# One signal of TensorE for each expert step, and expert outputs in two PSUM banks

## The reference

```python
g = t @ gate_w.T + gate_b                      # t: 2816 x 192 normed tokens, 16 experts
vals, idx = jax.lax.top_k(g, 4)
w = jax.nn.softmax(vals, axis=-1) / K
full_w = zeros((T, E)).at[arange(T)[:, None], idx].set(w)
h = jnp.einsum('th,ehf->tef', t, w1) + b1      # 192 -> 384 (gate and linear half)
h = _swiglu(h)                                 # min(g,7) * sigmoid(1.702 g) * (clip(l)+1)
y = jnp.einsum('tei,eih->teh', h, w2) + b2     # 192 -> 192
out = jnp.einsum('teh,te->th', y, full_w) * K
```

## Time and profile before

| what | us |
|---|---|
| median of 3 plain runs | 689.53 (689.51 to 690.78) |
| profiled execution, span from first to last instruction | 774.6 |
| busy in it: PE, DVE, ACT, POOL | 435.0, 574.6, 541.6, 456.0 |
| start of the first and of the last hidden product | 467.8, 721.3 |
| last copy of `y_ps` begins | 735.1 |

### The profile page before, as it was taken

The page is one execution under the profiler, slowest core; times in us unless marked ns, Lnnn a source line. Parts: engine busy times, 40 slices in busy tenths (PEclk is TensorE's granted clock), DMA queues, the critical chain, the costliest instruction groups (busy, mean ns, idle before and its releaser), DMA issues.

```text
span 774.6 us, 14447 instructions
## 1 busy us (share of the span) xinstructions
PE 435.0 (56%) x3943; PEld 289.1 (37%) x3943; DVE 574.6 (74%) x1466; ACT 541.6 (70%) x905; POOL 456.0 (59%) x554
## 2 busy tenths in 40 slices
PE   0794343645546364464642223775787787868544
PEld 0242132333324233242331222554565555546333
DVE  3787897799998999989888853565576665656746
ACT  0065898999998989999897622454666666667564
POOL 9781726237488888978878546455455454545510
PEclk9998555555555555555555556777999899999769
DMA  9469999998002021210010115532544443441078
GB/s 185 52 145 307 318 318 294 317 298 243 6 28 77 29 77 45 67 36 20 26 35 25 35 54 114 109 82 78 116 105 90 88 90 86 106 88 45 2 273 327
DMA packets 149613, 93.65 MB, mean 121 GB/s; under 512 B 77122, under 2 KB 143643, under 8 KB 149538
## 3 DMA queue, kind: packets, MB, share of 16 engines
q1 hardware_dynamic: 139266, 75.04, 38.1%
q0 software_dynamic: 10272, 17.70, 7.1%
HBM read 23.61 MB, written 61.24 MB: 110 GB/s over the span
## 4 chain that ended last, share of the span: by engine, by line
ACT 32%; SPq 17%; PE 16%; issue 12%; another core or an unknown queue 9%; DVE 8%; POOL 2%; DMA 2%; DVEq 0%; ACTq 0%; POOLq 0%
SPq L483 7%; PE pX L1927 4%; PE pS L1911 3%; PE pP L1911 3%; SPq L475 3%; ACT S_sq L1015 2%; ACT L1015 2%; PE pX L1681 2%; ACT S_sq L1010 2%; ACT stage L1060 2%; ACT S_u L886 2%; ACT S_sq L987 2%; ACT pTs L992 2%; SPq L432 2%
## 5 line engine op out<-in xcount | busy, mean ns | idle before, releaser
L782 POOL DMA_INDIRECT expert_rows<-stage,dest x118 | 118.7, 1006 | 124.2 <-ACT stage L1045 48.7
L1600 DVE TENSOR_SCALAR arena<-pS 128x512 f32<-128x512 f32 x59 | 40.7, 689 | 74.8 <-remote 49.9
L1927 PE MATMUL pX<-w2s,stage 128*128 x472 | 64.4, 269 | 44.1 <-ACT stage L1045 39.9
L706 POOL DMA_INDIRECT region<-rows,slots x60 | 68.1, 1135 | 16.3 <-issue 15.7
L597 POOL TENSOR_TENSOR w1s<-stage,w1s 128x384 f16<-128x384 f32 (+8 forms) x72 | 59.5, 826 | 11.0 <-ACT w1s L866 5.8
L1927 PEld LDWEIGHTS pX<-w2s,stage 128*128 128x128 f16 x472 | 43.1, 105 | 60.5 <-issue 57.3
L1681 PE MATMUL pX<-arena,WA 128*128 128x384 f16 x86 | 34.4, 502 | 42.5 <-ACT arena L878 29.5
L1803 PE MATMUL pP<-idb,S_p 128*88 128x128 bf16 x192 | 25.8, 316 | 54.3 <-DVE S_p L1418 54.3
L1053 ACT ACTIVATE arena<-pS 64x256 f32<-64x256 f32 x59 | 22.1, 375 | 48.7 <-remote 16.5
L706 POOL DMA_INDIRECT region<-arena,slots x36 | 42.9, 1191 | 16.1 <-issue 8.4
L752 POOL CAST oq<-o 128x384 bf16<-128x384 int8 x24 | 25.3, 1056 | 45.5 <-ACT o L970 45.5
(11 more groups left out here) (445 smaller groups left out, 1688.5 us busy)
## 6 DMA issues: line engine op xcount, KB each, us to landing
region<-zrow SPq DMA_DIRECT2D x45, 800.0 KB
w1s<-expert_rows SPq DMA_DIRECT2D x16, 384.0 KB, 7.4
stage<-in_L_ffn_w_dram SPq DMA_DIRECT2D x24, 192.0 KB
stage<-in_L_ffn_w_dram SPq DMA_DIRECT2D x8, 384.0 KB
w2s<-expert_rows SPq DMA_DIRECT2D x8, 384.0 KB, 11.8
arena<-in_x_dram SPq DMA_DIRECT2D x4, 672.0 KB
expert_rows<-stage,dest POOLq DMA_INDIRECT x118
out_dram<-xsel SPq DMA_DIRECT2D x8, 198.0 KB
```

The lines of the kernel that those rows point to most:

```text
L706: pool.indirect_dma_start(region_rows, bass.IndirectOffsetOnAxis(ap=slots[q % 3][:, i, m:m + 1], axis=0), rows[q % 3][:, i, :].bitcast(I16 ...
L782: pool.indirect_dma_start(y_dram, bass.IndirectOffsetOnAxis(ap=dest[(st - 7) % 8][:, j:j + 1], axis=0), ysb[b][:, j, :], None, bounds_chec ...
L1600: dve.tensor_scalar(lin[r], hidLC[r], -6.0 * XS * WS, 8.0 * XS * WS, ALU.max, ALU.min).then_inc(s["l_done"], 1)
L1927: ins = pe.matmul(y_ps[:, j, :], lhs, w2s[:, kind, bass.ds(k_, 1), :].rearrange("p o f -> p (o f)"), start=n == 0, stop=n == 4)
```

## The change

PE's three signals on the windows go. One signal, `products_done`, stands behind everything that a slot does, on the last output product (or on the last hidden one, where the slot has no output products). Every reader of `h_ready`, `hl_ready` and `mm2_done` now waits for `products_done` with the slot's number. The two gelus then wait for the same count, so the second wait goes. From block `Y_APART` = 7 on, outputs of odd blocks go to `pO` and those of even blocks to `pX` (`y_ps(n)`); before that all go to `pX`. From block 8 on, PE waits for the copy of two blocks before. At block 7, the first in `pO`, PE waits for `own_ready` 2, since `pO` holds the last group's table till then. The number and order of matmuls, copies and DMAs is the same.

```diff
-        y_ps = pX[:, 0:2 * C].rearrange("p (j c) -> p j c", j=2)
+        y_banks = [bank[:, 0:2 * C].rearrange("p (j c) -> p j c", j=2) for bank in (pX, pO)]
+        def y_ps(n):
+            return y_banks[n % 2 if n >= Y_APART else 0]
...
+        Y_APART = SPREAD_AT
...
 # SP, load_step
-                    sp.wait_ge(s["hl_ready"], p - (UNROLL - 1))
+                    sp.wait_ge(s["products_done"], p - (UNROLL - 1))
...
 # ACT, gate_values
-                    act.wait_ge(s["mm2_done"], p - 5)
+                    act.wait_ge(s["products_done"], p - 2)
...
-                    act.activation(ysb[b], y_ps, ACT.Copy, scale=1.0 / (XS * WS * WS)).then_inc(s["y_out"], 1)
+                    act.activation(ysb[b], y_ps(st - 6), ACT.Copy, scale=1.0 / (XS * WS * WS)).then_inc(s["y_out"], 1)
                 if active(st, 2):
-                    act.wait_ge(s["h_ready"], p * 2 - 3)
+                    act.wait_ge(s["products_done"], p - 1)
...
-                    act.wait_ge(s["h_ready"], p * 2 - 2)
...
-                        act.wait_ge(s["mm2_done"], p - 6)
+                        act.wait_ge(s["products_done"], p - 3)
...
-                        act.wait_ge(s["hl_ready"], p - 3)
+                        act.wait_ge(s["products_done"], p - 3)
...
 # DVE, expert_values
-                        dve.wait_ge(s["mm2_done"], p - 7)
+                        dve.wait_ge(s["products_done"], p - 4)
...
-                    dve.wait_ge(s["hl_ready"], p - 1)
+                    dve.wait_ge(s["products_done"], p - 1)
...
 # PE, products
-                        ins.then_inc(s["hl_ready" if dst is hidL[r] else "h_ready"], 1)
...
+                    if st - 5 == Y_APART:
+                        pe.wait_ge(s["own_ready"], 2)
                     if st >= 6:
-                        pe.wait_ge(s["y_out"], p - 5)
+                        pe.wait_ge(s["y_out"], p - 5 if st - 5 <= Y_APART else p - 6)
...
-                            ins = pe.matmul(y_ps[:, j, :], lhs, ...
+                            ins = pe.matmul(y_ps(st - 5)[:, j, :], lhs, ...
...
-                    ins.then_inc(s["mm2_done"], 1)
+                if active(st, 2) or active(st, 5):
+                    ins.then_inc(s["products_done"], 1)
```

More of the change, by code:

```diff
@@ L315, in audio_tower @@
             counted tabs_spread table_cols tabs_ready own_ready weights_ready
-            h_ready hl_ready l_done gs_ready a_ready hi_ready lo_ready lot_ready ave_ready te_copied mm2_done y_out dest_ready
+            products_done l_done gs_ready a_ready hi_ready lo_ready lot_ready ave_ready te_copied y_out dest_ready
             tails_zeroed rk_done scales_ready summed tile_out combined out_stored""".split()
@@ L1926, in products @@
                                                          (av[g][:, 2, tok], 2), (avE[g][:, tok], 3))):
-                            ins = pe.matmul(y_ps[:, j, :], lhs, w2s[:, kind, bass.ds(k_, 1), :].rearrange("p o f -> p (o f)"),
+                            ins = pe.matmul(y_ps(st - 5)[:, j, :], lhs, w2s[:, kind, bass.ds(k_, 1), :].rearrange("p o f -> p (o f)"),
                                             start=n == 0, stop=n == 4)
-                    ins.then_inc(s["mm2_done"], 1)
+                if active(st, 2) or active(st, 5):
+                    ins.then_inc(s["products_done"], 1)
             step_slots(pe, products, last_quad)
```

## The result

| kernel | median, us | runs |
|---|---|---|
| before | 689.85 | 4 (689.51 to 690.78) |
| after | 697.03 | 4 (696.07 to 698.91) |

The ratio is 1.0109, with a 95% interval of 1.0086 to 1.0131: 7.2 us slower. Predicted were 699, so +9.5.

What follows compares the result with a forecast made beforehand. Four engines all need 2.5 to 2.7 us a slot, with late signals blamed on profiling. Terms 5.2 + 4 + 1.3 = 10.5, less overlap 9.5, on 689.5 gave 699 us; range 684 to 707.

Steps and rivals of the forecast that it cites:

- The signals are worth nothing on PE: Three signals fewer on PE's matmuls in each slot: gain taken as 0, upper bound 0.13 us a slot.
- Rival 2: Each signal costs PE or its receiver something, so fewer are faster: 682 to 688 us; chance 0.06.
- The loop: Last 43 blocks: late signal, gelu, `tEb`, PE over two slots; 2.76 us a slot against 2.64, +5.2 us.
- Slots 6 to 12: Early slots with one output bank take 4.04 us each; partly covered, +4 us, bounds 0 and 9.8.
- The end: Last slots: later signal delays the y copies some 1.8 us, second bank closes POOL's 0.46 gap; +1.3 us.
- How the profiled execution stands to the median: Span 774.6 us against median 689.53: late signals in the expert steps taken as due to profiling, slots priced without them.
- Rival 1: Late signals partly remain in plain runs, so the second bank saves PE's y-copy waits: 677 to 686 us; chance 0.16.
- Rival 3: The new loop is covered by plain slots of 2.76 us or more, or TensorE at 1.2 GHz: 689 to 694; chance 0.18.
- What would show it: Signs in the profile after: PE waits for `tEb`, y-copy waits only before block 8, late signals still there, span well over median.

Runs made afterwards that it cites:

- noscat_before: The kernel before, without POOL's two indirect scatters of each expert step; 699.53 us on chip 9, where the kernel before took 782.73.
- noscat_after: The kernel after, without POOL's two indirect scatters of each expert step; 706.98 us on chip 9.
- noscat_te_first: The kernel after with `tEb` copied right behind the y copy, ahead of the gelus, and without POOL's expert scatters; 699.82 us on chip 9.
- banks_only: The kernel before with its four signals kept and outputs in two banks from block 7; 764.78 us, ratio 0.9848 on chip 14.

## Why the prediction was right, and where it was not

- **The signals are worth nothing on PE** (taken: 0, bound 7.7 us). Right. Over blocks 30 to 56 the fifteen hidden products start 0.56, 0.55 and 0.44 us apart by window in `noscat_before` with four signals and in `noscat_after` with one. A removed signal changed the distance of these starts by under 5 ns. The Trainium skill's 26 ns for each increment ("TensorE: Matmul & The Clock Gate", The cost: per-tile semaphore tail), which it gives for the tail after a burst of tiles, is not to be seen between these products. Rival 2 is out.
- **The loop** (taken: 2.76 against 2.64, 5.2 us over the last blocks). The mechanism and the difference were right: 116.69 to 121.38 is 4.7 us, 0.11 a slot. About 1 us of it, in blocks 21 to 28, is not this loop, as `noscat_te_first` shows. Both levels were some 0.13 too low (2.78 and 2.89 measured). Slots of before at 2.73 are PE's alone, whose own sum was set at 2.65 from borders of 0.20 and 0.12 in one slot; the mean ones are 0.24 and 0.13, and windows 0.56, 0.55, 0.44, halves 0.49 and 0.33, in sum 2.74. The same sum goes into the loop: 0.28 + 1.96 + 0.42 + 0.39 + 2.62 = 5.67, or 2.83 a slot (2.61 to 2.62 are the slot to its last product, 5.52 was predicted for the whole); 2.85 is measured from block 30 on. An error common to both sides cancelled, which is luck. The strict change of long and short slots is not there (2.76, 2.92, 2.82 in a row). For blocks 25 to 27 slots take 3.0 to 3.3 us in all four kernels.
- **Slots 6 to 12** (taken: +4, bounds 0 and 9.8). Measured +2.35 (67.53 to 69.88). The slot of 4.04 is there, 4.08 to 4.13. But there are four of them, not seven, and in their place `noscat_before` had 2.46, 5.41, 3.42 and 3.50 us, so these four cost 1.65 us. But late signals lengthen some of those (the 2.56 and 2.08 us shown above), and in the timed condition they should be shorter. With slots of 2.73 in their place the four would cost 5.5 us (16.42 - 4 x 2.73, my estimate), so the +4 is neither confirmed nor refuted there; that condition has no trace of before.
- **The end** (taken: +1.3). Measured -0.8 (12.76 to 11.92), made of two parts: the second bank alone -2.65, the later signal +1.8. The 1.8 is what was predicted; the second bank was priced at POOL's gap of 0.46, while PE's and ACT's gaps at the table loads were the ones it closed. This holds for kernels without POOL's scatters; with them it was not measured apart.
- The parts sum to 4.7 + 2.35 - 0.8 = 6.2 in the traces, and the medians differ by 7.45; the rest lies within the spread of `noscat_before`. Predicted 9.5 against 7.2: in this pair the excess is in the early slots and the end. How the 7.2 of the timed pair divide stays open for the early slots.
- **How the profiled execution stands to the median.** This step failed. I took late signals "for something that goes with being profiled". The kernel before took 770 to 785 us in every plain run on chips 14, 4 and 9, and in each of the twelve experiments the profiled execution lies among the plain ones (all 2.1 to 2.2 us over their span). The trace of before and its plain times must have come from different conditions; on which chip that trace was taken no run shows. What saved the number was luck in the consequence: to price slots without late signals, which is the condition that the timed pair happened to have. With late signals the forecast of +9.5 would not have held: on chip 4 single runs of after lie from 13 us below before's median to 10 above.
- **Rival 1** was right for the other condition: 11 us from the second bank alone, in `banks_only`. That this is near its 13 is chance, for the 13 was what of the late signals it thought plain runs could still hold (3 + 10), not the price of the wait. With one signal the gain is lost again in most runs.
- **Rival 3**'s slot of nearly 4.8 us at the lower clock is more than the two rows named for it give (2.65 x 1.03 / 0.61 = 4.5). It did not come to it: the granted clock was 1.00 from block 16 on.
- **What would show it.** Hidden products do wait for `tEb` (by the distance of 0.39, not by the view of waits), output products for the y copy before block 8 alone, the gelu starts 0.28 behind the last product: all as written. "Late signals during POOL's scatters should be there as before, and the span well over the median" was wrong, for the reason above.

## What to carry to other kernels

When several engines need nearly the same time per step (here 2.5 to 2.7 us), moving one signal to the end of the step makes a loop through every instruction that is queued behind its reader; add that loop up over as many steps as it spans, and move the last link (here `tEb`) ahead of the reader instead, which brought the slots back to those of before from block 30 on, and the whole time by 7 us. If the span of the profiled execution is far from the plain times, take it for another condition of the machine and run the kernel before again beside the change before reading anything off the difference of two traces. The version to try is two output banks with four signals: 0.985 to 0.988 where signals are late, and no slower, perhaps 3 us faster, where they are not (the latter without POOL's expert scatters alone; it was not run in the timed condition).

## What the runs showed that was not expected

- One and the same kernel took 689.9 us in the timed pair and 776 to 783 us on three chips in the experiments. Without POOL's expert scatters it took 699.5 us on one of those three, so 83 us there hang on them. POOL itself issues them 1.28 us apart in either condition.
- In that condition PE is hit on both sides: ACT waited 3.42 us for a signal from it, and its own instructions start late ("issue" 0.49 us at 606.52).
- There, after's runs are in two clusters some 18 us apart (764.8 to 768.0 and 782.5 to 787.8), and those with unread signals lie in both and between them; with `tEb` first or with four signals they are in one. Not explained.
